# First-layer steps of a feature-map attention phase in blocks of 3, 3 and 2 per two periods

## What is computed

```python
def prep(t):                                             # t: tokens x 16 heads x 16
    h1 = jnp.tanh(jnp.einsum('bshd,do->bsho', t, w1) + b1)   # w1: 16 x 256
    return jnp.einsum('bsho,on->bshn', h1, w2) + b2          # w2: 256 x 16
qp, kp = prep(Q), prep(K)
...
q1 = jnp.einsum('bshn,nm->bshm', qc, Hc)
qe = jnp.real(jnp.einsum('hcb,bshn->cshn', R, q1))
qq = jnp.sum(qe ** 2, -1)
attn = softmax(s / s)                                    # s = qq * kk
out = jnp.einsum('bijh,bjhd->bihd', attn, V).reshape(Bn, Sn, Dn)
```

## Time and profile before

| what | value |
| --- | --- |
| runs (3) | 1496.75 to 1497.97 us, median 1497.88 |
| span of the profiled execution | 1494.7 us |
| PE / PEld / DVE / ACT / POOL busy | 1463.1 / 1040.2 / 1139.0 / 845.7 / 391.0 us |
| first-layer steps | 17.8 to 324.5 us of the span |
| tanh (line 689) | 256, median 1114 ns, 18.4 to 326.0 us |
| granted TensorE clock | 1.00 of full speed in that stretch |

### The profile page before, as it was taken

The page is one execution under the profiler, slowest core; times in us unless marked ns, Lnnn a source line. Parts: engine busy times, 40 slices in busy tenths (PEclk is TensorE's granted clock), DMA queues, the critical chain, the costliest instruction groups (busy, mean ns, idle before and its releaser), DMA issues.

```text
span 1494.7 us, 28692 instructions
## 1 busy us (share of the span) xinstructions
PE 1463.1 (98%) x11013; PEld 1040.2 (70%) x11013; DVE 1139.0 (76%) x2313; ACT 845.7 (57%) x1123; POOL 391.0 (26%) x424
## 2 busy tenths in 40 slices
PE   8999999999999999999999999999999999999998
PEld 5333343435666666666656888898989898898987
DVE  6445544369899999999967888788686878788686
ACT  5888899976888888888873431223222221222221
POOL 1000000124546777666453420000000000000001
PEclk9999999999999999999999999999999999999999
DMA  7765556556656656656652201110010101110001
GB/s 151 149 116 114 106 114 126 94 103 114 108 85 104 109 80 110 107 79 96 98 169 71 78 15 31 28 29 18 22 33 15 40 18 29 28 30 15 21 23 29
DMA packets 89888, 108.62 MB, mean 73 GB/s; under 512 B 18373, under 2 KB 58321, under 8 KB 89753
## 3 DMA queue, kind: packets, MB, share of 16 engines
q1 hardware_dynamic: 89624, 106.61, 37.6%
q10 hardware_dynamic: 128, 0.20, 0.0%
HBM read 26.00 MB, written 4.19 MB: 20 GB/s over the span
## 4 chain that ended last, share of the span: by engine, by line
PE 85%; DVE 7%; ACT 3%; issue 2%; POOL 1%; DMA 1%; SPq 1%; POOLq 0%; DVEq 0%; ACTq 0%
PE ps L109 81%; PE ps L1440 2%; ACT H L689 2%; DVE NM L1670 1%; ACT PX L1612 1%; PE ps L1402 1%; PE ps L1448 1%; SPq L119 1%; DVE EE L856 0%; POOL X L1855 0%; PE ps L1373 0%; DVE GH L2563 0%; DVE GF L2557 0%; DVE GH L2561 0%; DMA ST<-QS 0%
## 5 line engine op out<-in xcount | busy, mean ns | idle before, releaser
L1670 DVE TENSOR_REDUCE NM<-ps 128x4 f32<-128x1024 f32 x256 | 307.3, 1218 | 23.3 <-PE ps L109 22.6
L1612 ACT ACTIVATE PX<-ps 128x1024 f32<-128x1024 f32 x256 | 262.2, 1024 | 72.3 <-PE ps L109 70.5
L689 ACT ACTIVATE H<-ps,b1c 128x1024 f32<-128x1024 f32 x256 | 267.7, 1119 | 39.7 <-PE ps L109 38.2
L2332 ACT ACTIVATE GF<-ps,cols 128x512 f32<-128x512 f32 x128 | 87.2, 687 | 222.1 <-PE ps L109 208.6
L109 PE MATMUL ps<-XC,W_sw_w 128*128 128x512 f32 x768 | 187.1, 393 | 0.0
L109 PEld LDWEIGHTS ps<-XC,W_sw_w 128*128 128x128 f32 x768 | 140.1, 188 | 27.5
L2683 POOL TENSOR_SCALAR RSc<-AGc 128x4 f32<-128x4 f32 x23 | 6.0, 259 | 570.9 <-DVE AGc L2447 570.9
L2327 ACT ACTIVATE GF<-ps 128x512 f32<-128x512 f32 x64 | 38.1, 596 | 185.6 <-PE ps L109 185.6
L2563 DVE TENSOR_TENSOR GH<-GF,GH 128x512 fp32r<-128x512 f32 x192 | 133.9, 697 | 6.6
L109 PE MATMUL ps<-PX,VT 128*32 128x256 f32 x2048 | 137.1, 385 | 0.1
L109 PE MATMUL ps<-KT,QT 48*128 48x512 f32 x512 | 127.6, 496 | 1.9 <-DVE NM L1670 0.9
(11 more groups left out here) (258 smaller groups left out, 2498.1 us busy)
## 6 DMA issues: line engine op xcount, KB each, us to landing
KT<-KS SPq DMA_DIRECT2D x128, 192.0 KB, 4.7
ST<-QS SPq DMA_DIRECT2D x254, 96.0 KB, 2.8
QT<-XSb SPq DMA_DIRECT2D x128, 96.0 KB, 4.2
XR<-TT SPq DMA_DIRECT2D x352, 32.0 KB, 1.9
XT<-in_xT_dram SPq DMA_DIRECT2D x8, 512.0 KB, 4.0
raw_a<-in_x_dram SPq DMA_DIRECT2D x8, 512.0 KB, 4.4
CR<-in_ctxT_dram SPq DMA_DIRECT2D x8, 512.0 KB, 6.0
out_dram<-X SPq DMA_DIRECT2D x7, 512.0 KB, 2.9
```

Source lines behind the costliest of these rows:

```text
L689: e.activation(H1[s % 8][:, :, :], PP[s % 3][:, :, :], ACT.Tanh, bias=b1c[:, half:half + 1], scale=1.0).then_inc(act_th, 1)
L1612: e.activation(PX[s % 3][:, :, :, :], PP[2][:, :, :].rearrange("p g (c q) -> p g c q", c=2), ACT.Exp, bias=0.0, scale=0.25).then_inc(act_e ...
L1670: e.tensor_reduce(NM[u % 2][:, qc, :, :, i], PP[qc][:, :, :].rearrange("p g (m k) -> p g m k", m=2), AX.X, ALU.max, negate=True).then_inc( ...
L2332: e.activation(g[:, :], o, f, bias=cols[:, col:col + 1], scale=1.0).then_inc(act_g, 1)
```

## The change

TensorE's order of the w1 steps changes; no other engine's code does. In periods 0 and 1 all stays. From period 2 on an even period issues three steps (4J to 4J+2) ahead of the middle work and none behind it. The fourth, 4J+3, opens the following odd period, which issues 4J-1, 4J, 4J+1 ahead and 4J+2, 4J+3 behind. w2(J - 1) keeps its place at the end of each period. The tanh has had its bias pointer before as after.

```diff
+    def ahead(J):
+
+        if J >= NJ:
+            return ()
+        if J < 2:
+            return range(4 * J, 4 * J + 2)
+        return range(4 * J - J % 2, 4 * J + 3 - J % 2)
+
+    def behind(J):
+
+        if J >= NJ or (J > 1 and J % 2 == 0):
+            return ()
+        return range(4 * J + 2, 4 * J + 4)
...
         for J in PERIODS:
-            for r in range(2):
-                if J < NJ:
-                    if J == 0 and r == 0:
-                        w.wait_ge(dve_w2p, 1)
-                    w1(4 * J + r)
+            for s in ahead(J):
+                if s == 0:
+                    w.wait_ge(dve_w2p, 1)
+                w1(s)
...
-            for r in range(2, 4):
-                if J < NJ:
-                    if J == 0 and r == 3:
-                        w.wait_ge(*free[6])
-                        busy(6, 3)
-                    w1(4 * J + r)
+            for s in behind(J):
+                if s == 3:
+                    w.wait_ge(*free[6])
+                    busy(6, 3)
+                w1(s)
```

## The result

| | before | after |
| --- | --- | --- |
| runs | 11, median 1497.60 us (1495.88 to 1503.51) | 11, median 1504.46 us (1501.30 to 1509.04) |
| ratio | 1 | 1.0046, 95% interval 1.0033 to 1.0059 |
| span of the profiled execution | 1494.7 us | 1502.1 us |
| start of period 56 | 286.25 us | 287.88 us |
| last tanh starts | 325.99 us | 331.39 us |

What follows compares the result with a forecast made beforehand. TensorE sets the pace, with ScalarE under it by less than a microsecond a period. Periods 2 to 55 add 0.3 us, the late ones 3.6: about +4, span 1498.7; with 3.2 to the median, forecast 1501.8, range 1498.3 to 1504.5.

Steps and rivals of the forecast that it cites:

- The mechanism: Even periods' third w1 step waits for the last tanh issued; a wait over 0.08 us costs its pair more than saved.
- block of three: Three w1 steps on TensorE in one block: 0.90 us start to start, against 0.66 for a block of two.
- period 49 step for step: Periods 48 and 49: last step held to 7.31 by a tanh behind a square, pair 9.59 against 9.00, loss 0.59.
- The rule on tiling modes: TensorE: switching tiling mode drains it, about 0.15 us seen, so fewer w1 blocks alone would mean a faster kernel.
- The lost cover: Periods 14, 22, 30: no w1 block hides w2's wait for VectorE to return bank 6 after attend; loss 0.43 us.
- means2 in bank 6: Periods 10 and 26: the w1 block covering w2's wait for VectorE's eviction goes; loss 0.99 us.
- Pair 2: Periods 2 and 3: a gain, given as 0.93 us together with periods 4 and 5.
- Pair 44: Periods 44 and 45, with a direct square and project in the odd period: loss 0.50 us.
- Pair 60: Periods 60 and 61, which hold steps of the next phase: loss 0.30 us.
- The 3.2 from span to run time: Whole kernel: median of the runs lies 3.2 us above the profiled span, added to span 1498.7 to give 1502.
- Rival 3: Each stall delays VectorE's evictions, making bank 6 or 7 late; 0.1 us at 31 even blocks: +7, 1505 us; chance 0.10.
- the named signs: Trace after: period 56 within 1 us of 286.25, first score product 4 us behind 327.17, set idles and waits in periods 12 to 49.

Runs made afterwards that it cites:

- e11: The changed kernel run once more, unaltered, in a later session: median 1504.94 us over 11 runs, best 1500.62.
- e2: The changed kernel with the new order in periods 56 to 63 only, the old order elsewhere: median 1501.44 us, ratio 1.0026 to the kernel before.
- e1: The changed kernel with the new order in periods 2 to 55 only, 56 to 63 as before: median 1500.41 us, ratio 1.0013 to the kernel before.
- e6: The kernel before (old order) with each tanh from step 8 on over half its columns: one execution, period 56 starting at 283.37 us, span 1496.9.
- e7: The changed kernel (new order) with each tanh from step 8 on over half its columns: one execution, period 56 starting at 275.72 us, span 1483.6.
- e4: The changed kernel with the new order only in the pairs of periods starting at 10, 14, 22, 26, 30: median 1500.30 us, ratio 1.0009 to the kernel before.

## Why the prediction was right, and where it was not

**Direction, place and size at full clock: right.** The forecast was +4 us on the span, all of it before the first score product. At full clock the two traces of this kernel have 3.7 there: 5.4 less one stretch of 1.7 in the changed kernel, 7.1 less two in e11. Of it 3.6 (e2) to 3.8 (the changed kernel) lie in periods 56 to 63, where the forecast had 3.64, and 0.1 (e1) to 0.25 (the changed kernel) in 2 to 55, where it had +0.3. The times of whole runs say the same less sharply. In e11's session the best runs are 4.2 apart (1500.62 and 1496.39), and those with a clock of 0.999 or more 2.8 (medians 1501.07 of two and 1498.24 of 18).

**The mechanism: right.** Third steps wait for tanh 4J-1 and last steps for a tanh behind a square; with tanh halved the same order gains 7.65 us by period 56 (e6, e7). The steps of the sum held: block of three 0.89, release 1.16 behind the tanh, period 49 step for step.

**The rule on tiling modes: right in sign, and beside the point.** With ScalarE fast, fewer w1 blocks make TensorE faster (e6, e7). The Trainium skill, TensorEngine Tiling (Array Packing), Key Properties, says that a change of tiling mode drains TensorE; the sign agrees, but no run here tells a drain from another cost of starting a block. What the rule doesn't see is the engine that has to keep up.

**The lost cover: wrong.** The step "A w1 block stood inside that time and hid; now nothing does. Loss 0.43" gave nearly the right number to the wrong cause. In e4 the cover is gone and the loss is 0.02. The eviction sets w2's start in both orders; the loss comes from the waiting third step that delays attend, which the same line of the sum has as 1.44 instead of 0.99. Measured it is 1.33 (83.98 to 85.31), and the loss 0.35. For means2 in bank 6 the cover is worth nothing either: of the 0.86 measured (forecast 0.99) 0.41 is the longer blocks (e4) and the rest the waiting third step.

**Terms mis-sized.** Pair 2: -0.50 forecast, +0.27 measured, for a wait of 1.04 on VectorE's eviction at the start that the walk had no term for. Pair 44: +0.50 forecast, +0.14 measured. Pair 60: +0.30 and +0.59. With the smaller misses they nearly cancel; that part is luck. The 3.2 from span to run time was mis-sized too: in every run listed with its span the time lies 1.75 to 1.95 above the span of the same execution, and the rest of the 3.2 is that the profiled execution was quicker than the median one. With 1.8 the sum gives 1500.5.

**The clock: missing.** The prediction took the full clock from the earlier trace rows as given and priced the new pauses at their length. The 6.9 us between the medians are about 4 at full clock; the rest goes with a mean clock of 0.9970, where one stretch of 1.7 us lowers it by about 0.001. That put the median at 1504.46 instead of at 1501.8, inside the range by 0.04 us, and that it stayed inside is luck: in e11's session the same kernel had 1504.94. I named no rival for it. Rival 3 has about this size, 1505, but its mechanism, 0.1 more at each of 31 even blocks, is not in the table of pairs. The stretch is also why two of the named signs failed: period 56 started 1.6 behind 286.25 and not within 1, and the first score product 5.4 later and not 4. Two more were a little off: the last step of 49 has an idle time of 0.30 and not 0.45, and ScalarE is idle for 0.92 before the tanh of 49 and not for over 1.

## What to carry to other kernels

Count both sides of a hand-over before reordering one of them: a producer's block may grow only as far as the consumer has emptied the buffers by then, and with three buffers the third step of a block needs the last tanh that was issued. Where some periods gain and others lose, take the order period by period: the same edit confined to 16 of 31 pairs turned +0.46% into -0.42%. And walk the queues with measured start-to-start times, in the old order first; here that was good to 0.1 us in 22 of 30 pairs.

## What the runs showed of the hardware that I had not expected

A pause of TensorE can cost more than itself. After idle times of 0.17 and 0.79 us within 3 us, the granted clock fell from 2.4 to 1.2 GHz and w2 took 3.2 to 3.5 us instead of 1.92. This happened at five of the 12 places with both idle times in periods 14, 22 and 30, at least once in each of the four profiles; each such stretch cost 1.7 us. It happened at none of the nine places with the second idle time alone, and at none of the six where three matmuls of no use filled it. But it did not happen in period 62 either, with idle times of 1.03, 0.17 and 0.78, in any of six traces; so the runs show where the clock fell and that it did not fall with the pause filled, and not what decides it. The Trainium skill, TensorE: Matmul & The Clock Gate, section "A second HAM failure mode: psum-queue depth-cycling", tells of a kernel whose frequent small idles between groups of matmuls let the clock swing between its two levels. The traces here agree in so far as two idles of under a microsecond went before each fall; how often they have to come, no run here shows.
